# Loads of weight codes, scales and output codes issued in other slots of a unit

## The reference

```python
w = (codes - 8.0) * repeat(scales, 128, axis=0)          # 4-bit weights, held as int32
q, k, v = h @ w_q, h @ w_k, h @ w_v                       # h = layernorm(x)
q, k = rope(q), rope(k)
scores = q @ k.T * 128 ** -0.5 + causal_mask
out = softmax(scores) @ v                                 # per head
x = x + layernorm(out @ w_o)                              # w_o: codes and scales too
x = x + layernorm(ffn(layernorm(x)))                      # int weights, hidden width 1376
```

## Time and profile before

| what | value |
|---|---|
| median of 3 runs | 1536.74 us |
| the profiled execution's own time | 1538.01 us |
| its span, first to last instruction | 1536.2 us |
| PE, DVE, ACT, POOL busy, share of the span | 93%, 72%, 64%, 60% |
| mean granted clock of TensorE | 0.979 of full speed |
| DMA engines, mean busy share in the attention part | 8 or 9 tenths |

### The profile page before, as it was taken

The page is one execution under the profiler, slowest core; times in us unless marked ns, Lnnn a source line. Parts: engine busy times, 40 slices in busy tenths (PEclk is TensorE's granted clock), DMA queues, the critical chain, the costliest instruction groups (busy, mean ns, idle before and its releaser), DMA issues.

```text
span 1536.2 us, 40725 instructions
## 1 busy us (share of the span) xinstructions
PE 1431.4 (93%) x11104; PEld 852.4 (55%) x11104; DVE 1105.0 (72%) x2500; ACT 987.4 (64%) x2582; POOL 919.0 (60%) x642
## 2 busy tenths in 40 slices
PE   4779799999999999999999999999999976999998
PEld 2445466556656665656656555665666553554543
DVE  7846477677768777777777777777777786776754
ACT  2576577777768777777777777777777763332321
POOL 2566577777767776777777777777777751010100
PEclk8999899999999999999999999999999988999999
DMA  8279989888888988998899989988988864011000
GB/s 269 63 161 176 170 166 163 165 160 168 165 159 165 164 161 155 173 161 169 158 165 171 172 159 167 171 169 154 167 164 163 150 117 95 15 48 42 15 28 28
DMA packets 522615, 217.15 MB, mean 141 GB/s; under 512 B 478944, under 2 KB 480704, under 8 KB 522432
## 3 DMA queue, kind: packets, MB, share of 16 engines
q1 hardware_dynamic: 519968, 210.53, 70.8%
q0 software_dynamic: 2464, 4.23, 1.6%
HBM read 55.32 MB, written 4.19 MB: 39 GB/s over the span
## 4 chain that ended last, share of the span: by engine, by line
PE 46%; POOL 12%; DMA 11%; issue 10%; SPq 10%; ACT 9%; DVE 1%; POOLq 0%; ACTq 0%; DVEq 0%
POOL p_lo L504 6%; DMA ot<-o_parts 5%; DMA swap<-other 4%; SPq L384 4%; PE ps_s L1027 4%; PE ps_s L1028 4%; POOL rot L488 4%; PE ps_p L792 4%; PE ps_p L793 4%; PE ps_p L794 4%; PE ps_p L816 3%; PE ps_p L817 3%; ACT p_hi L637 3%; PE ps_p L1041 2%; PE ps_p L1042 2%
## 5 line engine op out<-in xcount | busy, mean ns | idle before, releaser
L1118 DVE SCALAR_TENSOR_TENSOR y<-ps_p,wo_scale,y 128x512 f32<-128x512 f32 x512 | 381.0, 745 | 84.7 <-PE ps_p L817 70.8
L504 POOL TENSOR_TENSOR p_lo<-prob,p_hi 128x1280 f16<-128x1280 f32 x128 | 343.3, 2682 | 164.3 <-ACT p_hi L637 157.6
L628 ACT ACTIVATE prob<-prob,exp_bias 128x512 f32<-128x512 f32 (+3 forms) x512 | 285.6, 558 | 12.4
L1131 DVE CUSTOM_DVE_ANT_0 prob<-ps_s,mask 128x512 f32<-128x512 f32 (+3 forms) x512 | 236.8, 482 | 35.5 <-PE ps_s L831 30.2
L792 PE MATMUL ps_p<-x_hi,w_hi 128*128 128x512 f16 x640 | 244.9, 383 | 2.9 <-DVE w_lo L1052 1.5
L816 PE MATMUL ps_p<-ot,wo 128*128 128x512 f16 x512 | 199.4, 389 | 51.5 <-DMA ot<-o_parts 46.0
L793 PE MATMUL ps_p<-x_lo,w_hi 128*128 128x512 f16 x640 | 244.7, 382 | 0.0
L794 PE MATMUL ps_p<-x_hi,w_lo 128*128 128x512 f16 x640 | 244.3, 382 | 0.0
L488 POOL TENSOR_TENSOR rot<-rot,swap 128x512 f32<-128x512 f32 x160 | 203.2, 1278 | 51.3 <-DMA swap<-other 51.3
L845 PE MATMUL ps_o<-v_hi,ffn_w 128*128 128x128 f16 x1280 | 222.4, 220 | 10.1 <-DVE rot L1106 3.9
L846 PE MATMUL ps_o<-v_lo,ffn_w 128*128 128x128 f16 x1280 | 222.3, 220 | 0.0
(11 more groups left out here) (100 smaller groups left out, 2949.3 us busy)
## 6 DMA issues: line engine op xcount, KB each, us to landing
swap<-other SPq DMA_DIRECT2D x320, 128.0 KB, 3.1
w_code<-w_codes SPq DMA_DIRECT2D x36, 384.0 KB, 3.7
w_scale<-w_scales SPq DMA_DIRECT2D x36, 384.0 KB, 5.0
o_code<-o_codes SPq DMA_DIRECT2D x35, 256.0 KB, 2.9
swap<-x SPq DMA_DIRECT2D x16, 256.0 KB, 2.8
out<-z SPq DMA_DIRECT2D x16, 256.0 KB, 2.0
ffn_w<-x SPq DMA_DIRECT2D x3, 1024.0 KB, 9.8
ffn_w<-p_hi SPq DMA_TRANSPOSE x128, 3.6
```

The costliest lines, as they stand in the source:

```text
L504: pool.tensor_tensor(p_lo[:, :], prob[:, hp, :], p_hi[:, :], ALU.subtract).then_inc(p_lod, 1)
L628: act.activation(prob[:, hp, a:a + w], prob[:, hp, a:a + w], ACT.Exp, bias=exp_bias[:, hp, i:i + 1], scale=-1.0, accum_out=exp_sum[:, hp, ...
L1118: dve.scalar_tensor_tensor(tile, ps_p[:, bank, :], scale, tile, ALU.mult, ALU.add).then_inc(o_add, 1)
L1131: dve.tensor_tensor_reduce(prob[:, hp, P_AT[i]:P_AT[i] + w], ps_s[:, bank, col:col + w], mask[:, S - w:], -SCORE_SCALE, NO_MINIMUM, ALU.ad ...
```

## The change

In SyncE's `unit`, `load_o(U + HG)` (output codes) moves from the second step of a unit to the first, and `load_w(U + 6, r)` (weight codes and scales) from the second to the fourth. The first unit keeps its four loads of output codes, one in each step. The waits inside both functions and all buffers stay, and no other engine's program changes.

```diff
--- before.py
+++ after.py
@@ -436,9 +436,9 @@
                         turn_o(n - 2, h % 2)
                     if first:
                         load_o(h + 1)
-                    elif h == 1 and not last:
+                    elif h == 0 and not last:
                         load_o(U + HG)
-                    if h == 1 and more:
+                    if h == 3 and more:
                         load_w(U + 6, r)
                     if last:
                         if h == 0:
```

## The result

The changed kernel takes 1545.47 us (median of 7 runs, 1541.24 to 1552.0) against 1538.25 (1535.62 to 1543.7) for the kernel before on the same chip: a ratio of 1.005 [1.0032, 1.0068]. It is slower by half a per cent, where 1531.6 had been forecast. The profiled execution took 1545.38 us.

What follows compares the result with a forecast made beforehand. TensorE was taken as the bound, with a second loop over swap, rotation and `p_hi` setting 37 us a unit. -16.1 + 5.0 + 3.2 + 1.3 + 1.5 = -5.1 us gave 1531.6 us, range 1523 to 1545.

Steps and rivals of the forecast that it cites:

- First and fourth steps: TensorE's waits there for `ot` vanish, -16.1 us in 27 units; the fourth step's own transpose costs +1.3 us.
- The account of the stall: Third step: GpSimd waits for a swap behind the loads, 1.5 us a unit, delaying `p_hi` and later `ot`.
- Second steps: Waits stay and grow to 0.5 us each, +5.0 us; weight loads delay the first step's `ot` transpose, +3.2 us.
- FFN loads: At the start, unit 1's weight load now falls among them and lengthens unit 2's wait, +1.5 us.
- their waits were fulfilled long before, so no new wait stands in SyncE's list: Both moved loads still land a step or more ahead of their readers; no cost counted.
- the 11.4 us after loop branches: Rest of TensorE's 36.0 us of stalls, mostly late starts of softmax @ v behind its branches; taken as unchanged.
- Rival 3: Slower: backlog delays the first step's `ot` transpose by 1.0 us a unit, +18.7 us in sum, 1555.4 us; chance 0.15.

Runs made afterwards that it cites:

- e5: Against the kernel before: output codes loaded in the first step; weights in the fourth step of even units, the second step of odd ones; 1522.8 us, ratio 0.991.
- e1: Against the kernel before: only the load of output codes moved, to the first step; weight loads stay in the second; 1520.5 us, ratio 0.9882.
- e11: Against the kernel before: output codes loaded in the first step, weights in the third; 1521.05 us, ratio 0.9912.
- e8: Against the kernel before: output codes loaded in the first step and `w_low` moved earlier in VectorE's fourth step; 1513.86 us, ratio 0.9857.
- e3: Changed kernel with VectorE's `w_low` moved from the fourth step's end to behind the reciprocal of that step; 1537.23 us, ratio 0.9991 to the kernel before.
- e10: Kernel before with only `w_low` moved earlier in VectorE's fourth step; 1530.27 us, ratio 0.9962.
- e6: Against the kernel before: output codes loaded in the first step; weights in the fourth step of odd units, the second step of even ones; 1544.49 us, ratio 1.0038.
- e2: Against the kernel before: only the weight loads moved, to the fourth step; output codes stay in the second; 1545.67 us, ratio 1.0045.
- e9: Changed kernel with the loops of VectorE and TensorE both begun two units later; 1564.77 us, ratio 1.0193 to the kernel before.
- e7: Changed kernel with only VectorE's loop begun two units later; 1531.4 us, ratio 0.9958 to the kernel before.

## Why the prediction was wrong

*First and fourth steps* (forecast -16.1, and +1.3 for the fourth step's transpose). Right, but for the six first steps behind VectorE's branch. First and fourth steps together stood 16.8 us above bare; without the 12.1 us of those six, counted below, 2.4 are left: -14.4 against -14.8. That those six too would be bare without the load is what e5 shows (7.63 each). The account of the stall, 1.5 us a unit in the loop over swap, rotation and `p_hi`, holds, with one correction: it needs all of the 1 MB. e1 shows that 768 KB in the same slot are hidden.

*Second steps* (+5.0 and +3.2). They went from 8.7 to 15.2 us, +6.5 against +8.2. Both reasons given are real, but their sizes were wrong and the sum came near by luck. With the third step's stall gone and no weight load ahead of the first step's transpose, second steps cost 7.4 us (e1) or 9.4 (e11) and not 13.5, so the +5.0 was -1.3 to +0.7. The backlog behind the weight loads made the rest, 15.2 - 9.4 = 5.8 to 15.2 - 7.4 = 7.8 us, where 3.2 was forecast. e8 and e3 say the same: `w_low` early takes 5.3 of the 7.4 us away in e8, and only 2.0 of the 15.2 in e3. The Trainium skill (SBUF — State Buffer, "SBUF: two separate sides") has GpSimd and a VectorE operation with two SBUF inputs exclude each other for a whole instruction. The trace agrees both ways: 3.35 instead of 2.62 us for `p_lo` where it comes second, 3.17 instead of 0.95 for `w_lo` where it does.

*FFN loads* (+1.5). The wait in unit 2, beside the earlier trace rows:

```profile
PE ps_p L816 <- DMA ot<-o_parts: 13.2, 1, 13.2
```

+0.9; in e1, e8, e10 and e11, whose `load_w` is elsewhere, it is 12.2 or 12.3.

*What failed* is a sentence that priced a part at nothing: "their waits were fulfilled long before, so no new wait stands in SyncE's list", together with the 11.4 us after loop branches "which I leave as it is". Moving 768 KB to the end of a unit was priced by what stands behind them in SyncE's list alone: a swap and a transpose. The code of VectorE comes by DMA too, is in no engine's list, and is wanted once in four units in just that step. It added 12.1 us in six first steps and 3.3 in two second steps at a lower clock, +15.4 where 0 was forecast. -14.4 + 6.5 + 15.4 is +7.5 for the 27 units, where 6.8 was measured; the sums of steps are good to some tenths each. Rival 3, the slower one, had the right sign and the wrong mechanism: the backlog reached the transpose by 0.2 to 0.3 us a unit and not by 1.0, and with first and fourth steps at -14.4 that alone would have left the kernel faster.

*What the trace of before could have told.* VectorE's pieces were in it, and `y` started 6.16 to 6.92 us into these six steps already. In two of them (units 6 and 18, 8.23 and 8.25 us long) the step already ended 1.33 us behind `y`. There was little or no cover left: a delay of 2 us in the pieces had to be TensorE's. That a load on SyncE's queue would delay them could not be read there.

## What to carry over

Before a large load is moved, look at what else comes by DMA in the new slot, the fetch of code after a loop branch among it: find the steps behind each engine's branch, and see how late its first instructions there already are. A load that is hidden in one unit may not be in the first unit of a pass, so a moved transfer is priced over a whole pass of the longest loop. And where two loads stand together, try each move alone: here one half won 1.2%, and the other lost more than that again.

## What the runs showed of the hardware

- A fetch of code can come as late as the end of a load on another queue. With 768 KB on SyncE's queue the 8 KB piece of VectorE's code came 0.2 us after the load's last packet in all six such steps of e6, 2 us later than without it; in two steps of the changed kernel it came amid the load. The Trainium skill (DMA: Bandwidth & Descriptors, "Queues, rings and completion order") has each DMA engine take turns between queues packet by packet, and puts some 9 to 17 descriptors into a packet. Each of the two weight loads is 128 rows of 3072 bytes in the trace, 8 for each of 16 DMA engines on the mean, so by that count (an estimate) a piece could wait for most of a load and the rule would still hold; the near equal counts of the earlier trace rows agree with taking turns. No run here shows what a turn holds. Whether the piece is asked for late or served late, the trace doesn't tell.
- Which of two engines waits for the other is decided by less than half a microsecond. `p_lo` 0.27 us ahead of `w_lo` makes VectorE's 0.95 us instruction 3.17 us long; the other way round GpSimd's 2.62 become 3.35.
- TensorE's two longest stops in the changed kernel (first steps 2.50 and 2.63 us too long) were followed by a lower clock, 11.85 us at 0.86 for a second step without idle time, and the four shorter ones (up to 2.06 us) by steps at full clock. The length of a stop doesn't decide it: in e2 first steps 2.58 and 2.78 us too long are followed by second steps of 10.21, and in e6, where all six are 2.49 to 2.88 too long, four are followed by a lower clock and two are not. In e9 the five steps with a stop of 3.9 to 4.7 us have a mean clock of 0.75 or 0.76 and take 13.6 to 14.2 us.
- A late fetch of code isn't always felt: with VectorE's branch moved, the pieces are as late and `y` doesn't wait (e7). That another part of the code falls into each piece there is a guess.
- With TensorE's branch moved too, TensorE stands still 3.9 to 4.7 us inside a group of matmuls in five first steps of five, until 1.2 to 1.5 us after a 16 KB packet of another queue has landed (e9, +1.9%).
